# Sixteen multiplications of a cleared tile ahead of the first projection of a four-layer cross-attention kernel

## The chip, the cores and the metric

The kernel runs on one core of a Trainium2 chip. The core has a matrix engine (TensorE, PE in the profile), a vector engine (DVE), a scalar engine (ACT), GpSimd (POOL) and a sync engine (SP), which issues most of the DMAs. The metric is the device time of one execution in microseconds (us); lower is better.

## The reference

The input `x` is 128 sequences of 64 tokens of width 128, the context is 128 sequences of 64 tokens of width 256. Four cross-attention layers follow on one another, all over the same context. The first has 16 heads of width 64, a bias on four columns of the logits and an output bias; the other three have a norm ahead, 16 query heads of width 8 and 4 key and value heads. In short:

```python
# layer 0
q = x @ Wq; k = ctx @ Wk; v = ctx @ Wv                 # 128->1024, 256->1024, 256->1024
logits = einsum('bhqd,bhkd->bhqk', q, k) * 64 ** -0.5 + col_bias
x = softmax(logits) @ v  ->  reshape @ Wo + bo + x
# layers 1, 2, 3
xn = x * rsqrt(mean(x * x) + 1e-5) * norm_w
q = xn @ wq; k = ctx @ wk; v = ctx @ wv                # 128->128, 256->32, 256->32
x = x + softmax(q k^T / sqrt(8)) @ v @ wo
```

Everything is float32, in the reference and in the kernel.

## The kernel before, in words

The 128 sequences are cut into 32 groups of 4 (256 tokens each; `g` from 0 to 31). One group goes through all four layers in SBUF: `cT` holds its context transposed, `xT` its running output, `KT`, `V`, `K3`, `KB` and `VB` its keys and values, `QT` its queries, and four tiles `E[s][u]` of 128x512 its scores. Three groups are under way at a time (`s = g % 3`).

The work is cut into steps named `(kind, g, l, u)`: `k`, `v`, `k3`, `q0` are projections from the loaded inputs, `s` the scores, `t` the transposes of the softmax, `pv0` and `pv` the product with the values, `wo0` and `wo` the output projection, `x2` and `q` the norm and the query of a later layer. The order of these steps on each engine is written out by tables of numbers (`PE_TIME`, `ACT_TIME` and so on, sorted into `PE_ORDER`, `ACT_ORDER`, `DVE_ORDER`, `POOL_ORDER`, `SP_ORDER`). The engines meet at semaphores: an event such as `p_ev` counts the finished steps of a kind, and `w.wait_ge` waits for one. The change touches none of the tables.

At the start, SP issues the loads in this order: `cT` of group 0, three quarters of `wk0` (the key weights), `xq` of group 0, `wq0`, `wv` in parts, and then the rest. ACT issues the fourth quarter of `wk0` (quarter 1, the one that TensorE uses first) at L1054, then the token indices, `iota`, the masks `mk` and the identity. GpSimd clears `KB` and `VB`. The vector engine waits for the small loads of ACT's queue (`l_b`) and then computes the column bias (`vector_setup`, L1161 to L1174). TensorE starts with the four `k` steps of group 0 (L928), each 4 matmuls with a moving operand of 256 columns; the first of them waits for `cT` and for quarter 1 of `wk0`. Then come the `q0` steps (L955), two `v` steps (L940) and the scores (L966), on whose end the vector engine's first `add` (L1198) waits.

The program's matmul on float32 operands stands in the trace as two weight loads and two matmuls: the 16 of the `k` steps of group 0 are 32 rows there.

Of the kernel before, what the change touches and what calls it, by code (L numbers as in the profile page):

```python
# [671 lines left out]
def xattn_kernel(nc, t):  # L672
    with ExitStack() as ctx:
        def sb(name, shape, dt=F32):
            return ctx.enter_context(nc.sbuf_tensor(name, shape, dt))

        def of(order, *kinds):
            return [st for st in order if st[0] in kinds]

        def signal(name, events, inc=1):  # L680
            return Signal(ctx, nc, name, events, inc)

        psum = ctx.enter_context(nc.psum_tensor("psum", [128, 8, 512], F32))
# [25 lines left out]
        E = [[sb(f"E{s}_{u}", [128, 512]) for u in range(4)] for s in range(NS)]  # L709
# [36 lines left out]
        for st in of(PE_ORDER, *ON_ACT, *ON_DVE, "s", "t"):  # L746
            _, g, l, u = st
# [37 lines left out]
        d_setup = signal("d_setup", range(40))  # L785
        d_w = signal("d_w", range(3))
        g_one = signal("g_one", range(3))
        d_lr = signal("d_lr", of(DVE_ORDER, "lr"))
        p_ev = signal("p_ev", of(PE_ORDER, *ON_ACT, *ON_DVE))
        p_s = signal("p_s", of(PE_ORDER, "s"))  # L790
# [119 lines left out]

        def tensor_program(e):
            w = Engine(e)

            for st in PE_ORDER:
                kind, g, l, u = st
                s, at = g % NS, bank_of[st]
# [5 lines left out]
                if kind == "k":  # L922
                    w.wait_ge(l_c[g % NC], g)
                    w.wait_ge(l_wk[u], u)
                    for jj in range(2):
                        j = 2 * u + jj
                        for k in range(2):
                            m = e.matmul(bank[:, T * jj:T * jj + T], wk0[:, k, 128 * j:128 * j + 128], cTg[:, k, :],  # L928
                                         start=(k == 0), stop=(k == 1))
                    m.then_inc(p_ev.sem, 1)  # L930
                elif kind == "v":
# [7 lines left out]
                    for k in range(2):  # L939
                        m = e.matmul(bank[:, 0:hi - lo], cTg[:, k, 128 * p:128 * p + 128], wv[:, k, lo:hi],  # L940
                                     start=(k == 0), stop=(k == 1))
                    m.then_inc(p_ev.sem, 1)
                elif kind == "k3":
                    w.wait_ge(l_c[g % NC], g)
                    w.wait_ge(l_sm, 13)
                    for k in range(2):
                        m = e.matmul(bank[0:96, 0:T], wks[:, k, :, :].rearrange("p l n -> p (l n)"), cTg[:, k, :],  # L947
                                     start=(k == 0), stop=(k == 1))
                    m.then_inc(p_ev.sem, 1)
                elif kind == "q0":  # L950
                    w.wait_ge(l_xq[g % NX], g)
                    w.wait_ge(l_wq, "l_wq")
                    for jj in range(2):
                        j = 2 * u + jj
                        m = e.matmul(bank[:, T * jj:T * jj + T], wq0[:, 128 * j:128 * j + 128], xq[g % NX][:, :],  # L955
                                     start=True, stop=True)
                    m.then_inc(p_ev.sem, 1)
                elif kind == "s" and l == 0:
                    w.wait_ge(a_ev, *[("q0", g, 0, i) for i in range(4)])
                    w.wait_ge(a_ev, *[("k", g, 0, i) for i in range(4)])  # L960
                    for jj in range(4):
                        for b2 in range(2):
                            for par in range(2):
                                for h2 in range(2):
# [3 lines left out]
                                                 start=True, stop=True)  # L968
                    m.then_inc(p_s.sem, 1)
                elif kind == "s":  # L970
                    w.wait_ge(a_ev, ("q", g, l, u))
                    w.wait_ge(l_kb[l - 1][g % 2], (g, 15))
                    for p in halves(g, u):
                        for b2 in range(2):
                            for r in range(4):
# [5 lines left out]
                                             start=True, stop=True)  # L981
# [169 lines left out]
        def vector_setup(e, w):  # L1151

            n = [0]

            def then(m):
                m.then_inc(d_setup.sem, 1)
                e.wait_ge(d_setup.sem, n[0] + 1)
                n[0] += 1

            w.wait_ge(l_b, 6)  # L1160
            then(e.tensor_copy(idf[:, 0, :], idx[:, :]))  # L1161
            then(e.tensor_scalar(idf[:, 1, :], idf[:, 0, :], 0.0, 64.0, ALU.is_lt, ALU.mult))
            then(e.tensor_tensor(idf[:, 0, :], idf[:, 0, :], idf[:, 1, :], ALU.add))
            for i in range(4):
                then(e.tensor_scalar(eq[:, i, :], iota[:, :], idf[:, 0, i:i + 1], None, ALU.is_equal))
            then(e.tensor_tensor(eq[:, 0, :], eq[:, 0, :], eq[:, 1, :], ALU.max))
            then(e.tensor_tensor(eq[:, 2, :], eq[:, 2, :], eq[:, 3, :], ALU.max))
            then(e.tensor_tensor(eq[:, 1, :], eq[:, 0, :], eq[:, 2, :], ALU.mult))
            then(e.tensor_tensor(eq[:, 0, :], eq[:, 0, :], eq[:, 1, :], ALU.subtract))
            then(e.tensor_scalar(mk[:, :], mk[:, :], -1.0, 1.0, ALU.mult, ALU.add))  # L1170
            then(e.tensor_scalar(mk[:, :], mk[:, :], -20.0, None, ALU.mult))
            then(e.tensor_scalar(bias[:, :], eq[:, 0, :], mk[:, 0:1], None, ALU.mult))
            then(e.tensor_scalar(eq[:, 2, :], eq[:, 2, :], mk[:, 1:2], None, ALU.mult))
            then(e.tensor_tensor(bias[:, :], bias[:, :], eq[:, 2, :], ALU.add))  # L1174
            return n[0]
# [2 lines left out]

        def vector_program(e):
            w = Engine(e)  # L1180
            assert vector_setup(e, w) == setup_steps
            scaled = False
            for st in DVE_ORDER:
# [75 lines left out]
        @block.tensor  # L1259
        def _(e):  # L1260
            tensor_program(e)
# [5 lines left out]
        @block.vector  # L1267
        def _(e):
            vector_program(e)
# [38 lines left out]
```

## Time and profile before

| | |
|---|---|
| median of 3 runs | 1388.01 us (1386.95 to 1388.95) |
| the profiled execution's own time | 1385.33 us |
| its span, first to last instruction | 1383.5 us |
| TensorE busy | 1360.6 us (98%) |
| first matmul starts at | 4.52 us |

The page gives busy time by engine, the chain of work that ended last, and the costliest groups of instructions. In the trace, times count from the span's start. A matmul's duration runs from its start until its result is out, so the durations of matmuls that follow on one another overlap: 32 matmuls of 379 ns each do not take 32 times 379 ns. The pace is read from the starts, or from the chain, which gives the time without the overlap. The column PEclk is the granted clock of TensorE as a share of 2.4 GHz: 1.00 is 2.4 GHz, 0.50 is 1.2 GHz.

### The profile page before, as it was taken

What the parts mean: (1) busy time and instruction counts of PE and PEld (TensorE: products, weight loads), DVE (VectorE), ACT (ScalarE), POOL (GpSimd) and SP (SyncE); (2) the same over time, 40 slices, a digit from 0 to 9 for tenths busy, and PEclk for the clock granted to TensorE, in tenths of its full rate; (3) what the DMA queues carried; (4) which work ended last, traced back from release to release, by engine and by line L of the source; (5) the groups of instructions that cost most, each with busy time, mean ns of one, the idle gap of its engine ahead of it and who ended that gap; (6) DMA issues with size and microseconds to landing.
All of it is one profiled execution on the core that took longest, in us unless ns stands there. A gap on an engine that the chain in (4) does not pass through costs nothing.

```text
span 1383.5 us, 58994 instructions
## 1 busy us (share of the span) xinstructions
PE 1360.6 (98%) x25464; PEld 1053.6 (76%) x25464; DVE 1064.0 (77%) x2257; ACT 1003.3 (73%) x2207; POOL 735.7 (53%) x852
## 2 busy tenths in 40 slices
PE   8999999999999999999999999999999999999996
PEld 6777777778777777777777777777777777777775
DVE  3488777977778877778877779777788777787876
ACT  3677777767777677777677777677776776767785
POOL 5355446555456545466554465455565544655643
PEclk9999999999999999999999999999999999999998
DMA  5010000110000010100101101100011011010000
GB/s 149 18 30 18 19 25 23 27 27 24 26 21 24 27 27 23 28 18 26 27 24 26 29 17 27 27 23 27 18 27 27 23 27 31 12 39 19 7 22 13
DMA packets 46003, 37.02 MB, mean 27 GB/s; under 512 B 17072, under 2 KB 41520, under 8 KB 45744
## 3 DMA queue, kind: packets, MB, share of 16 engines
q1 hardware_dynamic: 44576, 32.89, 8.9%
q8 instruction: 201, 3.29, 1.0%
q14 instruction: 58, 0.48, 0.1%
q10 hardware_dynamic: 1168, 0.36, 0.1%
HBM read 16.42 MB, written 4.19 MB: 15 GB/s over the span
## 4 chain that ended last, share of the span: by engine, by line
PE 94%; DVE 3%; ACT 2%; issue 1%; POOL 0%; DMA 0%; DVEq 0%; POOLq 0%
PE psum L940 18%; PE psum L928 16%; PE psum L995 10%; PE psum L1013 8%; PE psum L955 8%; PE psum L977 7%; PE psum L1041 7%; PE psum L1005 5%; PE psum L966 5%; PE psum L1049 4%; PE psum L1018 3%; PE psum L947 2%; PE psum L1024 2%; ACT E L1127 1%; DVE st L1211 1%
## 5 line engine op out<-in xcount | busy, mean ns | idle before, releaser
L887 POOL TENSOR_TENSOR E<-E,st 128x512 f32<-128x512 f32 x488 | 497.1, 1043 | 169.8 <-DVE st L1223 161.8
L1122 ACT ACTIVATE E<-E,inv 128x512 f32<-128x512 f32 x384 | 273.4, 722 | 136.7 <-DVE E L1215 135.3
L1211 DVE TENSOR_REDUCE st<-psum 128x8 f32<-128x512 f32 x372 | 240.2, 672 | 147.9 <-PE psum L977 147.7
L1220 DVE TENSOR_REDUCE st<-E 128x8 f32<-128x512 f32 x488 | 320.9, 664 | 34.1 <-ACT E L1115 27.1
L1127 ACT COPY E<-psum 128x512 f32<-128x512 f32 x512 | 275.1, 609 | 36.5 <-PE psum L995 36.3
L940 PE MATMUL psum<-wv,cT 128*128 128x374 f32 (+1 forms) x768 | 273.3, 486 | 0.0
L1215 DVE TENSOR_TENSOR E<-psum,st 128x512 f32<-128x512 f32 x372 | 248.1, 676 | 0.3
L928 PE MATMUL psum<-cT,wk 128*128 128x256 f32 x1024 | 241.9, 384 | 5.4 <-DMA wk<-in_L_xattn_Wk 4.5
L899 POOL TENSOR_TENSOR nt<-nt,powers 128x2 f32<-128x2 f32 (+1 forms) x102 | 19.9, 195 | 422.2 <-DVE nt L1250 401.4
L928 PEld LDWEIGHTS psum<-cT,wk 128*128 128x128 f32 x1024 | 192.7, 191 | 39.9 <-DMA cT<-in_ctx_t 4.5
L940 PEld LDWEIGHTS psum<-wv,cT 128*128 128x128 f32 x768 | 138.1, 189 | 73.2 <-ACT V L1083 8.5
L995 PE MATMUL psum<-ident,E 64*128 64x64 f32 x4096 | 157.4, 226 | 7.8 <-ACT E L1122 4.0
L883 POOL TENSOR_TENSOR E<-E,st 128x512 f32<-128x512 f32 x140 | 142.6, 1043 | 36.5 <-DVE st L1205 24.6
L995 PEld LDWEIGHTS psum<-ident,E 64*128 64x128 f32 x4096 | 138.8, 139 | 24.4 <-issue 12.6
L955 PE MATMUL psum<-xq,wq 128*128 128x256 f32 x512 | 129.0, 385 | 0.0
L1041 PEld LDWEIGHTS psum<-E,VB 128*32 128x32 f32 x6144 | 92.1, 110 | 37.4 <-issue 14.8
L1013 PE MATMUL psum<-QT,wo 128*128 128x256 f32 (+1 forms) x544 | 119.1, 372 | 0.0
L1083 ACT COPY V<-psum 128x374 f32<-128x374 f32 (+1 forms) x192 | 87.3, 457 | 42.7 <-PE psum L940 41.9
L1107 ACT ACTIVATE QT<-psum 128x512 f32<-128x512 f32 x128 | 75.9, 599 | 56.0 <-PE psum L955 47.7
L955 PEld LDWEIGHTS psum<-xq,wq 128*128 128x128 f32 x512 | 94.8, 190 | 23.1 <-issue 10.8
L977 PE MATMUL psum<-KB,QT 32*64 32x256 f32 x3072 | 109.7, 388 | 2.1 <-ACT QT L1146 1.0
L1041 PE MATMUL psum<-E,VB 128*32 128x64 f32 x6144 | 108.2, 221 | 0.4 <-ACT E L1127 0.2
(63 smaller groups left out, 1612.3 us busy)
## 6 DMA issues: line engine op xcount, KB each, us to landing
KB<-K SPq DMA_DIRECT2D x1536, 8.0 KB
cT<-in_ctx_t SPq DMA_DIRECT2D x32, 256.0 KB, 2.8
xq<-in_x_t SPq DMA_DIRECT2D x32, 128.0 KB, 2.1
out<-xT SPq DMA_DIRECT2D x30, 128.0 KB, 1.8
wk<-in_L_xattn_Wk SPq DMA_DIRECT2D x3, 256.0 KB, 5.6
wv<-in_L_xattn_Wv SPq DMA_DIRECT2D x2, 374.0 KB, 8.6
wq<-in_L_xattn_Wq SPq DMA_DIRECT2D x1, 512.0 KB, 7.6
wo<-in_L_xattn_Wo SPq DMA_DIRECT2D x1, 512.0 KB, 4.3
```

What stands on the lines that cost most here:

```text
L887: e.tensor_tensor(E3, E3, wide(stat[s][u][:, 16:24]), ALU.mult).then_inc(g_nrm.sem, 1)
L928: m = e.matmul(bank[:, T * jj:T * jj + T], wk0[:, k, 128 * j:128 * j + 128], cTg[:, k, :], start=(k == 0), stop=(k == 1))
L940: m = e.matmul(bank[:, 0:hi - lo], cTg[:, k, 128 * p:128 * p + 128], wv[:, k, lo:hi], start=(k == 0), stop=(k == 1))
L955: m = e.matmul(bank[:, T * jj:T * jj + T], wq0[:, 128 * j:128 * j + 128], xq[g % NX][:, :], start=True, stop=True)
L995: m = e.transpose(psum[:, at[2 * n + i], c:c + 64], E[s][2 * p + r][rows, 128 * k:128 * k + 128], ident[rows, rows])
L1013: m = e.matmul(bank[:, tokens], wo0[:, j, :], QT[s][:, j, tokens], start=(j == 0), stop=(j == 7))
L1041: m = e.matmul(bank[32 * r:32 * r + 32, 64 * b:64 * b + 64], VBg[:, b, c:c + 32], E[s][b][:, n:n + 64], start=(gp == 0), stop=(gp == 1))
L1122: e.activation(E[s][u][:, :], E[s][u][:, :], ACT.Exp, scale=inv[s][:, u // 2:u // 2 + 1]).then_inc(a_exp.sem, 1)
L1127: e.copy(E[s][u][:, :], psum[:, i, :]).then_inc(a_et.sem, 1)
L1211: e.tensor_reduce(stat[s][u][:, 0:8].rearrange("p (r h) -> p r h", r=2), scores_of[g, l, u], AX, ALU.max).then_inc(d_max.sem, 1)
L1215: e.tensor_tensor(pairs(E[s][u][:, :]), scores_of[g, l, u], stat[s][u][:, 0:8].rearrange("p (r h a) -> p r h a", r=2, a=1).to_broadcast([1 ...
L1220: e.tensor_reduce(stat[s][u][:, 8:16], heads(E[s][u][:, :]), AX, ALU.add).then_inc(d_sum.sem, 1)
```

## The change

The vector engine clears the first 128 columns of tile `E[0][0]` as its first instruction, and says so by a new semaphore `d_blank`. TensorE waits for it and then multiplies this 128x128 float32 piece by itself sixteen times, into the first 128 columns of PSUM bank 7. Nobody reads that result; the next matmul that is put into this bank starts afresh, and the first step that writes `E[0][0]` (the `add` of group 0) comes after TensorE's scores of group 0. Everything else stays.

```diff
@@ -785,6 +785,7 @@
         d_w = signal("d_w", range(3))
         g_one = signal("g_one", range(3))
+        d_blank = signal("d_blank", ["blank"])
@@ -910,7 +911,10 @@
         def tensor_program(e):
             w = Engine(e)
-
+            blank = E[0][0][:, 0:128]
+            w.wait_ge(d_blank, "blank")
+            for _ in range(16):
+                e.matmul(psum[:, 7, 0:128], blank, blank, start=True, stop=True)
             for st in PE_ORDER:
@@ -1178,6 +1182,7 @@
         def vector_program(e):
             w = Engine(e)
+            e.memset(E[0][0][:, 0:128], 0.0).then_inc(d_blank.sem, 1)
             assert vector_setup(e, w) == setup_steps
```

On TensorE, at the program's start, this stands before (`cT` is the context, `wk` the key weights; `l_wk1`, `l_wk2`, `l_wk0` are the landings of quarters of `wk`, `l_c0` that of `cT`):

```order
L1259 UNCONDITIONAL_BRANCH [waits barrier_Pool_Activation_PE_DVE_SP_release]
L928 MATMUL psum<-cT,wk 128x256 [waits l_wk1,l_c0]
L928 MATMUL psum<-cT,wk 128x256 x3
L928 MATMUL psum<-cT,wk 128x256 [waits l_wk2]
L928 MATMUL psum<-cT,wk 128x256 x3
```

And on TensorE at the same place with the change (`E_0` is the cleared tile; lines are 4 further down, and L932 is L928 of before):

```order
L1264 UNCONDITIONAL_BRANCH [waits barrier_Pool_Activation_PE_DVE_SP_release]
L917 MATMUL psum<-E_0 128x128 [waits d_blank]
L917 MATMUL psum<-E_0 128x128 x15
L932 MATMUL psum<-cT,wk 128x256 [waits l_wk1,l_c0]
L932 MATMUL psum<-cT,wk 128x256 x3
L932 MATMUL psum<-cT,wk 128x256 [waits l_wk2]
```

Sixteen matmuls now stand ahead of the wait for the loads; the order behind them is the same.

On the vector engine, at the program's start, before (`l_b` is the landing of the small loads; `idf` holds the token indices as floats):

```order
L1267 UNCONDITIONAL_BRANCH [waits barrier_Pool_Activation_PE_DVE_SP_release]
L1161 CAST idf<-idx 128x4 [waits l_b]
L1162 TENSOR_SCALAR idf<-idf 128x4 [waits d_setup]
```

And there with the change:

```order
L1272 UNCONDITIONAL_BRANCH [waits barrier_Pool_Activation_PE_DVE_SP_release]
L1185 MEMSET E_0 128x128
L1165 CAST idf<-idx 128x4 [waits l_b]
L1166 TENSOR_SCALAR idf<-idf 128x4 [waits d_setup]
```

The clearing stands ahead of the engine's wait for the loads and waits for nothing itself.

## Rows read from the trace of the kernel before

**Rows 1.** The page: busy time, share of the span, instructions; then the chain by engine.

```profile
PE 1360.6 (98%) x25464; PEld 1053.6 (76%) x25464; DVE 1064.0 (77%) x2257; ACT 1003.3 (73%) x2207; POOL 735.7 (53%) x852
...
PE 94%; DVE 3%; ACT 2%; issue 1%; POOL 0%; DMA 0%; DVEq 0%; POOLq 0%
```

**Rows 2.** The chain of waits, 0 to 40 us: start us, us, what.

```profile
0.74 3.64 DMA wk<-in_L_xattn_Wk
4.38 0.14 issue
4.52 8.63 PE psum L928 x32
13.15 3.45 PE psum L955 x16
16.60 2.51 PE psum L940 x8
19.11 1.14 PE psum L966 x64
...
20.35 1.29 DVE E L1198 x2
```

**Rows 3.** Timeline of TensorE, 0 to 22 us: start us, us, group [idle before].

```profile
4.52 8.63 PE L928 MATMUL psum<-cT,wk 128*128 128x256 f32 x32 [4.52 <-DMA wk<-in_L_xattn_Wk]
12.99 3.62 PE L955 MATMUL psum<-xq,wq 128*128 128x256 f32 x16
16.44 2.68 PE L940 MATMUL psum<-wv,cT 128*128 128x374 f32 x8
19.05 2.10 PE L966 MATMUL psum<-KT,QT 64*64 64x64 f32 x128
```

**Rows 4.** Line L928, 4 to 6 us: duration ns min/median/max, first and last start.

```profile
L928 PE MATMUL psum<-cT,wk x4: 634/634/764, 4.5 to 5.9; 128*128 128x256 f32 x4
```

**Rows 5.** Line L928, 7.4 to 7.8 us.

```profile
L928 PE MATMUL psum<-cT,wk x3: 380/544/634, 6.8 to 7.6; 128*128 128x256 f32 x3
```

**Rows 6.** Line L928, 8.2 to 8.6 us.

```profile
L928 PE MATMUL psum<-cT,wk x3: 379/379/379, 8.0 to 8.5; 128*128 128x256 f32 x3
```

**Rows 7.** Stretches: length, PE busy (instructions), PEclk, DMA share, GB/s.

```profile
0.00:4.52 4.52, 0.00 (x1) 1.00 0.59 167
4.52:5.52 1.00, 1.00 (x3) 1.00 0.28 72
```

**Rows 8.** The chain, 1290 to 1297 and 1330 to 1337 us, 128x128 moving operands.

```profile
1292.88 3.77 PE psum L1013 x32
```

**Rows 9.** Stretches at the end, columns as in rows 7.

```profile
1363.00:1370.00 7.00, 5.82 (x174) 1.00 0.07 21
1370.00:1372.30 2.30, 0.25 (x13) 1.00 0.00 0
1372.30:1373.86 1.56, 0.73 (x17) 0.68 0.00 0
1373.86:1378.77 4.91, 4.91 (x144) 0.50 0.03 7
1378.77:1380.25 1.48, 0.00 (x1) 0.69 0.00 0
...
1379.60:1379.70 0.10, 0.00 (x0) 0.55 0.00 0
```

**Rows 10.** Waits, 0 to 25 us: who waited for whom, us, times, longest.

```profile
DVE idf L1161 <- DMA mk<-in_mask_S_fk: 12.3, 1, 12.3
ACT KT L1075 <- PE psum L928: 4.2, 1, 4.2
DVE E L1198 <- PE psum L966: 4.0, 1, 4.0
```

**Rows 11.** Timeline of all engines, 0 to 22 us, as rows 3.

```profile
0.74 0.48 ACTq L1054 DMA_DIRECT2D wk<-in_L_xattn_Wk  x1
0.79 0.14 POOL L865 MEMSET ones<- 128x48 f32 x1
3.18 0.43 SPq L814 DMA_DIRECT2D wq<-in_L_xattn_Wq  x1
4.13 2.14 SPq L816 DMA_DIRECT2D wv<-in_L_xattn_Wv  x1
15.79 0.26 DVE L1173 TENSOR_SCALAR eq<-eq,mk 128x64 f32<-128x64 f32 x1
17.79 0.64 ACT L1075 COPY KT<-psum 128x512 f32<-128x512 f32 x1
```

**Rows 12.** DMA issues: KB each, median us from issue to landing.

```profile
wv<-in_L_xattn_Wv SPq DMA_DIRECT2D x2, 374.0 KB, 8.6
wq<-in_L_xattn_Wq SPq DMA_DIRECT2D x1, 512.0 KB, 7.6
```

**Rows 13.** The page's groups: out<-in xcount | busy, mean ns of one.

```profile
L872 POOL MEMSET KB<- 128x1024 f32 x6 | 5.4, 961 | 0.1
```

## The prediction

> **What bounds the kernel now.** I read four views, from the whole to the start. First the page: TensorE is busy for 98% of the span and 94% of the chain that ended last lies on it, while no other engine is over 77% [rows 1]. Whatever the change does must be done to TensorE's time. The change adds to the first microseconds and touches no table of the order, so the second view is the chain of waits of the first 40 us [rows 2]. The chain begins with a DMA, quarter 1 of wk, from 0.74 to 4.38 us. Then TensorE carries it without a break: the 32 matmuls of the key projection to 13.15, the query projection to 16.60, the values to 19.11, and half of the scores, whose end lets the vector engine start at 20.35. The wait list says the same from the other side: the vector engine had stood idle for 4.0 us when the scores came, and ACT for 4.2 us when the first keys came [rows 10]. So in this stretch a microsecond on TensorE is a microsecond of the kernel, both ways, and from 0.74 to 4.38 TensorE has nothing to do.
>
> The third view is the durations within the key projection. Its first matmuls take 634 to 764 ns each [rows 4], those after 8 us take 379 ns [rows 6], and the change from one to the other falls between the last long one, started at 6.8, and the first short one, started at 7.6 [rows 5]. The work is the same shape throughout. The pace shows what this is worth. The 16 matmuls of the query projection, same shape, take 3.45 us in the chain [rows 2], 0.216 us each. At that pace 32 of them would take 6.90 us. They took from 4.52 to 12.99, the start of the next group [rows 3], 8.47 us. The first ones therefore cost 8.47 - 6.90 = **1.57 us too much**. If a slow one takes twice the time (0.431 us), 1.57 / 0.216 = 7.3 of them were slow, which fills 7.3 x 0.431 = 3.1 us and ends at 7.6, where rows 5 has the change. So TensorE ran at 1.2 GHz for about 3.1 us from its first matmul and at 2.4 GHz from then on. A trap for the reader: the granted clock is printed as 1.00 in these very stretches [rows 7]; here the durations have to be believed. Where the clock column does move is the fourth view, the end of the kernel: after a stretch in which TensorE was at work for only 0.25 of 2.30 us, the clock fell to 0.50 and stayed there while TensorE was busy without a gap from 1373.86 to 1378.77; it came back at 1379.65 or so, 5.8 us after that work began [rows 9]. The two places give the two ends for how long work goes on at half clock: 3.1 and 5.8 us.
>
> **The change, part by part.**
>
> *The clearing on the vector engine.* One memset of 128x128. Nothing of this shape runs there before. From below, GpSimd's memset of 128x48 takes 0.14 us; the nearest on the vector engine is 0.26 us for 128x64 [rows 11]; from above, GpSimd's memset of eight times the width takes 0.96 us [rows 13]. I take 0.2 us, between the two nearest. The engine's next instruction waits until 12.3 us anyway [rows 10], so on that engine it costs nothing. The queues start at 0.74 [rows 11]; with 0.2 for the clearing and the 0.14 us that passed between the landing of wk and the first matmul [rows 2], the first added matmul starts at about 1.1 us (1.0 to 1.9 by the ends).
>
> *The sixteen matmuls.* They become 32 rows of weights 128x128 and 128 moving columns. This shape does stand in the trace: in the last groups' output projection, 32 such matmuls take 3.77 us at full clock [rows 8], 0.118 us each. That is more than half of 0.216: with so few columns the pace is not that of the columns alone, so I use this row and not half of the wider one. At half clock I take twice that, 0.236 us (if only the columns count it is 0.216). All at full clock they would take 3.8 us and end at 4.9; all at half clock 7.5 us and end at 8.7. The wait that they fill ends at 4.52. So they do not fit into the wait in either case; this is the central point of the sum.
>
> *The clock.* I take the same 3.1 us of work at half clock as before. It fits 3.1 / 0.236 = 13.1 of the 32; the clock is up at 1.1 + 3.1 = 4.2 us. The other 18.9 take 18.9 x 0.118 = 2.2 us. The added block ends at 1.1 + 3.1 + 2.2 = **6.4 us**.
>
> *The key projection.* It starts at 6.4 in place of 4.52, 1.9 us later, and runs at full clock: 6.90 us in place of 8.47, 1.57 us less. It ends at 13.3 in place of 12.99. **Sum: +1.9 - 1.57 = +0.3 us.**
>
> The Trainium skill, in "TensorE: Matmul & The Clock Gate", section "Part 1: The HAM clock gate", says that the array starts at half rate and that activity releases it, and that the warm-up is a budget of time, not of a number of matmuls. The trace agrees as far as it goes (3.1 us slow in rows 4 to 6). By this rule the change does not save the slow time but only spends it on work that nobody needs, and what is gained is only as much of it as lies in the wait; by a reading in which a number of matmuls (7 of them) releases the clock, it would be up at 1.1 + 7.3 x 0.236 = 2.8 us, the block would end at 2.8 + 24.7 x 0.118 = 5.7 us, and the sum would be -0.4 us.
>
> *What is late next.* A start 0.3 us later is carried on: the chain from L928 to the vector engine's add has no gap [rows 2]. If the projection ended earlier instead, two things could hold it: wq lands at 3.18 + 7.6 = 10.8 us and the second part of wv at 4.13 + 8.6 = 12.7 [rows 11, 12], needed at 12.99 and 16.44 [rows 3], so 1.6 us earlier would still do; and ACT's last copy of keys ends at 18.43 [rows 11], 0.6 us ahead of the scores, and moves with TensorE. So gain or loss reaches the scores whole. From there the same order runs with the same durations, and I give the remaining 1360 us no change.
>
> Against the profiled execution's own 1385.33 us (span 1383.5 and 1.8 around it) this makes 1385.6. The median of the runs shown is 2.7 us above the profiled execution, so the forecast on that scale is 1388.01 + 0.3 = **1388.3 us**. A measurement of this kernel can tell about 0.2%, 2.8 us, from no change; the forecast is a tenth of that.
>
> **The rivals.**
>
> *B, the clock comes late.* The end of the kernel shows 5.8 us of work at half clock before it rose [rows 9], and the rise may also be bound to the moment of 7.6 us and not to the work. With 5.8 us, 24.6 of the added matmuls are slow and 7.4 take 0.9 us: the block ends at 7.8, the projection at 14.7, +1.7 us. With a rise at 7.6, 27.5 slow and 4.5 fast: it ends at 8.1, +2.0 us. Against it: nothing says that the start is like the end. Time 1389.7 to 1390.0.
>
> *C, the other side: zeros do not raise the clock.* The change would then not do what it says. All 32 are slow, the block ends at 1.1 + 7.5 = 8.6 us, the key projection starts 4.1 us late and is as slow at first as before: **+4.1 us**, 1392.1, slower by 0.30%. It decides as soon as the block is slow to its end and the first real matmuls still take over 600 ns. For it: no row shows what zeros do. Against it: the durations of this trace change after a time of work on a fixed shape, and I know of no row in which the data mattered. The same page of the Trainium skill says in that section that all-zero operands do not trip another limiter, one for peak current with three or more busy cores; by it zeros change nothing on one core, and no run here shows that limiter.
>
> *D, the block fits.* If the added matmuls were done by 4.5 us with the clock up, the whole 1.57 us would be gained: 1386.4. It needs 32 matmuls in 3.4 us, 0.106 each from the first on, below the 0.118 of full clock [rows 8]. A part of it remains possible (a shape whose weights do not change may go faster than in rows 8; the clock may rise earlier): -0.4 to -1.6 us.
>
> *E, something further down the line.* 64 more instructions lie ahead on TensorE and 1% of the chain is issue [rows 1], so that small gaps elsewhere may fall differently, by up to some 3 us either way.
>
> **How the numbers follow.** Forecast (-0.4 to +1.0 us) 0.60; B 0.17; C 0.08; D 0.09; E 0.06. Faster by over 0.2% needs 2.8 us, more than all the slow time at the start holds; only E can give it: 0.04 with what I may have missed. Slower by over 0.2%: C nearly whole, and a share of E: 0.09. Within 0.2%: 0.87. The range takes in D whole and B whole and leaves out C; with the spread of the runs (about 1 us each way) that is 1385.8 to 1391.2.
>
> **What the changed profile would show.** A group of 32 matmuls at L917 from about 1.1 us; its durations long at first and short from about 4.2 us; the key projection (L932 there) starts at about 6.4 us with a median and maximum near 379 ns, and takes some 7.1 us in place of 8.63; the query projection starts at 13.3; the vector engine's first add at about 20.7 in place of 20.35. B shows a start of the key projection near 8 us; C shows it at 8.6 with durations of 634 ns; D shows it at 4.5. The forecast is wrong if the add's start moves by over 1 us, or if it does not move and the total does.

## The result, and the profile after

The changed kernel takes 1390.3 us in the median of 17 runs (1387.83 to 1392.93); the kernel before took 1387.55 in 17 runs beside it (1383.38 to 1388.95). The ratio is **1.0023, with a 95% interval from 1.0017 to 1.0030**: slower by 3.2 us (the two medians are 2.75 us apart). The forecast was 1388.3 with a range from 1385.8 to 1391.2. The time lies in the range, but the step up is ten times the +0.3 us of the sum. It stands just above the 0.2% from which the prediction called a time slower, the class that had been given 0.09; the interval reaches below that line.

The profiled execution of the changed kernel took 1392.03 us, its span is 1390.2, 6.7 us over that of before. Both profiled executions are unlike their medians, in opposite directions (1385.33 against 1387.55, 1392.03 against 1390.3), so that their difference overstates the change.

The start of the chain of waits of the changed kernel (start us, us, what); it answers to [rows 2]:

```profile
0.83 0.18 DVE E L1185
1.01 0.04 issue
1.05 6.72 PE psum L917 x32
7.77 6.91 PE psum L932 x32
14.68 3.45 PE psum L959 x16
18.13 2.51 PE psum L944 x8
20.64 1.14 PE psum L970 x64
...
21.88 1.29 DVE E L1203 x2
```

The clearing takes 0.18 us and the first added matmul starts at 1.05. The block takes 6.72 us and not 5.3. The key projection behind it takes 6.91 us, all at full clock, in place of 8.63. The first add starts at 21.88 in place of 20.35, 1.53 us later.

The durations in the block tell when the clock rose. Line L917 of the changed kernel, first from 6.4 to 7 us and then from 7.15 to 7.5 (duration in ns min/median/max, first and last start):

```profile
L917 PE MATMUL psum<-E x5: 348/421/421, 6.1 to 7.0; 128*128 128x128 f32 x5
```

```profile
L917 PE MATMUL psum<-E x6: 274/275/421, 6.8 to 7.5; 128*128 128x128 f32 x6
```

Until about 7.1 us each added matmul takes 421 ns, from then on 275. The engine had worked at 1.2 GHz for 6.1 us, in place of the 3.1 us of the profile before. It had seen nothing but zeros until then, so zeros do raise the clock.

That is 1.5 of 6.7 us. The rest is further down the line. The time that TensorE stood idle with nothing to release it (engine, line, "issue": us in total, times, longest) in the profile before, and then in the changed one:

```profile
PE psum L995 <- issue: 2.0, 4, 0.7
PE psum L1005 <- issue: 1.3, 3, 0.8
PE psum L977 <- issue: 0.6, 2, 0.5
```

```profile
PE psum L1045 <- issue: 2.5, 2, 1.5
PE psum L1009 <- issue: 2.4, 6, 0.7
PE psum L999 <- issue: 1.4, 3, 0.7
PE psum L981 <- issue: 0.6, 1, 0.6
PE psum L944 <- issue: 0.5, 1, 0.5
```

Together 3.9 us before and 7.4 after, and at other places. One such place lies inside a row of 32 equal matmuls. First the timeline of before, where the 32 follow on one another, then the same step of the changed kernel, which stops after 27:

```profile
73.95 1.12 PE L977 MATMUL psum<-KB,QT 32*64 32x256 f32 x32
```

```profile
75.48 1.10 PE L981 MATMUL psum<-KB,QT 32*64 32x256 f32 x27
77.19 0.65 PE L981 MATMUL psum<-KB,QT 32*64 32x256 f32 x5 [0.61 <-issue]
```

The kernel before has such places too. At this one the changed kernel has none. Timeline of before:

```profile
152.84 0.73 PE L1005 MATMUL psum<-E,V 64*64 64x64 f32 x33
154.38 0.69 PE L1005 MATMUL psum<-E,V 64*64 64x64 f32 x31 [0.81 <-issue]
```

and the same step of the changed kernel:

```profile
156.11 1.16 PE L1009 MATMUL psum<-E,V 64*64 64x64 f32 x64
```

A semaphore cannot be the cause in the midst of one step, since only its first matmul waits. What the places have in common shows when TensorE's rows (weight loads, matmuls and its own semaphore rows) are counted from the start of the trace, the first as 0. The matmul behind a gap of this kind of over 0.25 us is row 4801, 15042, 20674, 32450, 38082, 43714, 47554 or 50370 before, and row 1986, 4033, 9665, 20674, 21442, 27074, 38082, 38850, 46017, 46273 or 51138 after. Two of them stand in both lists (20674 with 0.25 and 0.62 us, 38082 with 0.26 in both). Divided by 256, each leaves 193 or 194, and so do all 116 gaps of this kind in the 14 profiles of this document. And the program's code is itself loaded by DMA, in 201 pieces. The page of the changed kernel, DMA queues (packets, MB, share of 16 engines):

```profile
q8 instruction: 201, 3.29, 1.0%
```

3.29 MB in 201 packets is 16 KB each; TensorE has about 51,500 rows, which is 201 times 256. At the gap before 77.19 us a piece of code came in between 74.42 and 75.81, and TensorE went on 1.4 us after that; at the one before 154.38 of the old profile, between 151.70 and 153.01, again 1.4 us ahead. In all 116 gaps it is 1.0 to 1.6 us. So I read the gaps like this: where a boundary between two pieces falls behind many short instructions, TensorE arrives at it before its code does. The change puts 64 rows ahead of everything (16 matmuls, each two weight loads and two matmuls), so that every later boundary falls 64 rows earlier in the program. That became theory 2, against theory 1, that only the start counts.

### The profile page after: what moved, and what is told of

The parts are those of the page before. It is cut to its first block, busy times and chain, and to the rows that moved or that the text cites. A ratio compares the mean times of both kernels' runs of the same rounds, so it can differ in the third digit from the quotient of the medians.

```text
span 1390.2 us, 59059 instructions
## 1 busy us (share of the span) xinstructions
PE 1366.8 (98%) x25496; PEld 1059.7 (76%) x25496; DVE 1065.2 (77%) x2258; ACT 1003.2 (72%) x2207; POOL 736.4 (53%) x852
## 3 DMA queue, kind: packets, MB, share of 16 engines
q8 instruction: 201, 3.29, 1.0%
## 4 chain that ended last, share of the span: by engine, by line
PE 94%; DVE 2%; ACT 2%; issue 1%; DMA 1%; POOL 0%; DVEq 0%; POOLq 0%
PE psum L944 17%; PE psum L932 16%; PE psum L999 10%; PE psum L1017 8%; PE psum L959 8%; PE psum L981 7%; PE psum L1045 7%; PE psum L1009 5%; PE psum L970 4%; PE psum L1053 4%; PE psum L1022 3%; PE psum L951 2%; PE psum L1028 1%; ACT E L1131 1%; ACT E L1126 1%
## 5 line engine op out<-in xcount | busy, mean ns | idle before, releaser
L932 PE MATMUL psum<-cT,wk 128*128 128x256 f32 x1024 | 240.2, 382 | 1.5 <-DMA cT<-in_ctx_t 1.5
L932 PEld LDWEIGHTS psum<-cT,wk 128*128 128x128 f32 x1024 | 191.6, 190 | 35.7 <-ACT K L1105 1.4
```

## Experiments

Each ratio is to the kernel before, timed beside it on the same chip: experiments 1 to 4 on one chip, 5 to 8 on a second, 9 to 12 on a third. Ratios of different chips meet only through the kernel before. "Tiny" stands for a matmul with 32x32 weights and 1 moving column: it puts the same four rows into the stream and takes little time (32 rows in 1.86 us, in experiment 2).

**1. The clearing and the wait alone.** Against the changed kernel:

```diff
-            for _ in range(16):
-                e.matmul(psum[:, 7, 0:128], blank, blank, start=True, stop=True)
```

> The clearing and TensorE's wait for it stay, the sixteen matmuls are gone. Theory 1 (only the start counts: the added block ends late and pushes the key projection back): no block, ratio to before 1.000, key projection starts at 4.5 us. Theory 2 (the 64 added rows in TensorE's stream shift all later code against the places, every 256 rows, at which code loading stalls it): no rows added, ratio 1.000 as well, idle time put down to issue 3.9 us as before. If it is slower by over 0.1%, the clearing or the wait costs and both are short of something.

Measured: ratio 1.0002 (0.9993 to 1.0011). The clearing and the wait cost nothing that the runs can tell. The profile taught something else, though. Its chain:

```profile
4.47 9.73 PE psum L930 x32
```

The key projection took 9.73 us here, 8.63 before, with nothing ahead of it in either. So the time at half clock is not the same in each execution; twice the excess over full clock, (9.73 - 6.91) x 2, is 5.6 us here, and (8.63 - 6.91) x 2 = 3.4 us before. And the issue idle time was 5.6 us, not 3.9, so one profile does not fix it to better than 2 us.

**2. Sixteen tiny ones.**

```diff
-                e.matmul(psum[:, 7, 0:128], blank, blank, start=True, stop=True)
+                e.matmul(psum[0:32, 7, 0:1], blank[0:32, 0:32], blank[0:32, 0:1], start=True, stop=True)
```

> The same 64 rows in TensorE's stream, but each matmul only 32x32 weights and 1 moving column, so that the block is over long before the loads land at 4.4 us. Theory 1: ratio 1.000, first add of the vector engine at 20.4 us. Theory 2: first add at 20.4 us too, but the stalls fall as in the changed kernel: TensorE's idle time put down to issue near 7 us in place of 3.9, ratio 1.001 to 1.002.

Measured: ratio **1.0022** (1.0013 to 1.0030), as much as the whole change. In its timeline the block is over at 2.9 us and the key projection starts on time:

```profile
1.05 1.86 PE L917 MATMUL psum<-E 32*32 32x1 f32 x32 [1.05 <-DVE E L1185]
4.45 2.04 PE L932 MATMUL psum<-cT,wk 128*128 128x256 f32 x4 [1.53 <-DMA wk<-in_L_xattn_Wk]
```

The issue idle time is 7.1 us, near the 7.4 of the changed kernel. Theory 1 is out: the key projection is not pushed back and the 3 us are there.

**3. Eight of the sixteen.** `range(16)` becomes `range(8)`.

> Eight of the sixteen matmuls: 16 rows at 0.21 us end at 4.5 us, just as the loads land; 32 rows are added to the stream. If the clock rises by work done (3.1 us of it), the key projection runs at full clock at once and the first add comes 1.5 us earlier than before (18.9 us). If it rises at a moment near 7.1 to 7.5 us whatever was done, the first add stays at 20.4. Theory 1: the ratio follows the add alone, 0.999 or 1.000. Theory 2: plus a change of the stalls for a shift of 32 rows, of either sign up to 2 us.

Measured: ratio 0.9990 (0.9981 to 1.0000). The first add starts at 19.37 us, the earliest of all, though not as early as the 18.9 expected for a clock that rises after 3.1 us of work. A load that the prediction did not name now holds TensorE for a moment, that of the output bias `bo`; the profiles of experiments 7 and 12 show it too, at 0.2 us:

```profile
21.81 1.10 PE L951 MATMUL psum<-cT,wks 128*96 128x256 f32 x4 [0.20 <-DMA bo<-in_L_xattn_bo]
```

**4. Ones in place of zeros.**

```diff
-            e.memset(E[0][0][:, 0:128], 0.0).then_inc(d_blank.sem, 1)
+            e.memset(E[0][0][:, 0:128], 1.0).then_inc(d_blank.sem, 1)
```

> The changed kernel with the tile set to 1.0 in place of 0.0. If zeros count as little work for the clock, the clock rises earlier than at 7.1 us, the block takes under 6.7 us and the kernel gains up to 1.5 us on the changed one. If the values do not matter, the block takes 6.7 us again and the ratio is that of the change, 1.002.

Measured: ratio 1.0021 (1.0012 to 1.0031), as with zeros. In the profiled execution the clock did rise earlier, at 4.2 us, and the block took 5.33 us, but experiment 1 has shown that this moment differs from execution to execution; the runs show no gain. The profile is worth its line, because it is the case that the prediction had worked out (block over at 6.4):

```profile
1.05 5.33 PE psum L917 x32
6.38 6.91 PE psum L932 x32
13.29 3.45 PE psum L959 x16
```

**5. Eight tiny ones.** As 2, with `range(8)`.

> Eight tiny matmuls (32x32 weights, 1 moving column) at the start: the 32 added rows of the eight-matmul kernel without its work. If that kernel's ratio of 0.999 came from the clock, this one stands at 1.000 or above; if it came from where the code boundaries fall with a shift of 32 rows, this one shows 0.999 too.

Measured: ratio 0.9991 (0.9982 to 1.0000). A shift of 32 rows seems to be a small gain by itself (the interval just reaches 1; experiment 11 gives 0.9992), so experiment 3 had not shown that the clock was its cause.

**6. Sixteen tiny ones at the end.** No block at the start; behind TensorE's last step:

```diff
+            w.wait_ge(d_ev, PE_ORDER[-1])
+            for _ in range(16):
+                e.matmul(psum[0:32, 7, 0:1], blank[0:32, 0:32], blank[0:32, 0:1], start=True, stop=True)
```

> The 64 rows of the sixteen tiny matmuls stand behind TensorE's last step in place of ahead of its first, after the vector engine's last result. Theory 2 (code position) says that no earlier instruction changes its place: ratio 1.000, stalls at the same rows as before. If the ratio is 1.002 again, it is the longer program as such, or its additional fetches, and not the position.

Measured: ratio 1.0003 (0.9993 to 1.0013). The same 64 rows cost nothing that the runs can tell where nothing stands behind them. It is what the rows stand ahead of, and not the length of the program.

**7. Two wide ones.**

```diff
-            for _ in range(16):
-                e.matmul(psum[:, 7, 0:128], blank, blank, start=True, stop=True)
+            wide_blank = blank.rearrange("p (a n) -> p a n", a=1).to_broadcast([128, 4, 128])
+            for _ in range(2):
+                e.matmul(psum[:, 7, :].rearrange("p (a n) -> p a n", a=4), blank, wide_blank, start=True, stop=True)
```

> Two matmuls with 512 moving columns (the cleared 128 repeated four times): 4 matmul rows at 0.85 us each at half clock, done at about 4.5 us as in the eight-matmul kernel, but only 8 rows are added to the stream. Theory 1 and 2 together: the clock part of the gain is there (first add on average 1.5 us earlier), and the shift is small; ratio 0.999, at best 0.998.

Measured: ratio 1.0005 (0.9993 to 1.0017). A miss. The start is as expected (block over at 4.7, first add at 19.56), but the gain is not in the total. Either a shift of 8 rows costs something, or the gain at the start was lost on the way; a shift of 8 rows without work was not run.

**8. Thirty-two tiny ones.** `range(32)`.

> Thirty-two tiny matmuls at the start, 128 rows added, done at about 4.6 us. Theory 2: stalls at other matmuls again; the sum of them differs from both before and the shift of 64. From the spacing of the instructions before I expect a shift of 128 to be as bad as that of 64 or worse: 1.002 to 1.003. Theory 1 (start only): 1.000.

Measured: ratio 1.0021 (1.0012 to 1.0031), as expected.

**9. Forty tiny ones.** `range(40)`. The shift was chosen from the spacing of TensorE's rows in the profiles, as the worst.

> Forty tiny matmuls, 160 rows added, done at about 5.3 us, 0.8 us after the loads. From the spacing of TensorE's rows in the profiles so far (256 rows to a piece of code, a stall where the 150 to 160 rows ahead of a boundary run in under 2.4 us) a shift of 160 rows is the worst of all: 4 to 6 us of stalls more than with no shift. Theory 2: ratio 1.003 to 1.005. Theory 1, the start only: 0.8 us, 1.0006.

Measured: ratio **1.0034** (1.0022 to 1.0046, from 6 runs where the others have 11 or 12), the highest of all, though the interval overlaps those of experiments 2 and 8. The 4 to 6 us of added gaps are not in its profile: the issue idle time is 6.8 us there, against 3.9 to 6.2 with no shift. The first add in its profile is at 21.25 us, within what kernels without a block show (below). The block ends at 5.4, some 0.9 us after the loads have landed, and more than that the start cannot explain.

**10 and 11. Eight real and eight tiny ones, beside each other.**

> The eight-matmul kernel once more, now beside its twin with eight tiny matmuls on the same chip. The profiles so far give the first add at 19.4 to 19.6 us where work fills the wait and at 20.4 to 22.2 where it does not, 1.7 us apart in the mean. If that is carried to the end, this kernel is 0.0012 below its twin; if it is lost on the way, they are equal.

> The twin: the same 32 rows without work. Theory 2: 0.999 again, from the place of the code alone, and 0.0012 above the kernel with eight real matmuls if the clock part is carried to the end.

Measured: **0.9978** (0.9970 to 0.9987) with the real ones, 0.9992 (0.9983 to 1.0002) with the tiny ones, 0.0014 or 1.9 us apart (the medians are 1382.62 and 1384.86 us). Their first adds (vector engine's timeline; the eight real ones first, then the tiny ones):

```profile
20.23 1.29 DVE L1203 TENSOR_TENSOR E<-psum,bias 128x512 f32<-128x512 f32 x2 [3.83 <-PE psum L970]
```

```profile
21.48 0.69 DVE L1203 TENSOR_TENSOR E<-psum,bias 128x512 f32<-128x512 f32 x1 [5.17 <-PE psum L970]
```

The two adds are 1.25 us apart, and the two spans, 1381.1 and 1382.4 us, still 1.3, with issue idle times of 3.5 and 3.3 us: in this pair of profiles the gain at the start is carried to the end. Eight real ones beat the kernel before here. The same pair in experiments 3 and 5 stood at 0.9990 and 0.9991, but on two chips. Taken together the real ones are ahead by 0.0008, about as much as the uncertainty of such a difference; that the clock part reaches the end is likely and not settled.

**12. Six of the sixteen.** `range(6)`.

> Six real matmuls, 24 rows added, done at 3.6 us, so that 0.9 us of the wait stays idle. By the spacing of the rows a shift of 24 is about as good as none (-0.5 us); the clock part is somewhat under that of eight, since the clock comes after work begun at 1.05 us and may count the idle stretch: -1.2 us. Ratio 0.999 (0.998 to 1.000).

Measured: ratio 1.0006 (0.9996 to 1.0016). A miss like experiment 7: the start has its gain (first add at 19.47), the total has not. My reading of the rows had the highest ratio at the shift of 160, as it came out, within the noise said above; it does not predict the small shifts.

The two parts, side by side. Position, from the kernels whose added rows do no work (experiments 1, 6; 5, 11; 2; 8; 9):

| rows ahead of the first step | 0 | 32 | 64 | 128 | 160 |
|---|---|---|---|---|---|
| ratio | 1.0002, 1.0003 | 0.9991, 0.9992 | 1.0022 | 1.0021 | 1.0034 |
| issue idle in the profiles, us | 5.6, 6.2 (before: 3.9) | 6.1, 3.3 | 7.1 | 7.1 | 6.8 |

Start, from the moment of the first add in each profile:

| what fills the wait | first add, us | mean |
|---|---|---|
| nothing, or tiny ones over by 2.9 (before, 1, 2, 5, 6, 11) | 20.35, 21.40, 21.11, 20.51, 22.23, 21.48 | 21.2 |
| six or eight real ones, or two wide ones (3, 7, 10, 12) | 19.37, 19.56, 20.23, 19.47 | 19.7 |
| sixteen real ones (the change, 4) | 21.88, 20.49 | 21.2 |

Experiments 8 and 9 stand in no row: their key projections start late, at 5.08 and 5.40 us (in 8 behind a load, in 9 behind the block), with the first add at 21.83 and 21.25. Within a row the adds lie up to 1.9 us apart, so the mean of two says little.

## Why the prediction was right or wrong

**The number.** That the time lies in the range is luck. The range reached that high because it took in rival B, a late clock, and the spread of the runs; what filled it was another mechanism. (Its ends are also not quite those of the sum: 1386.4 - 1 and 1390.0 + 1 are 1385.4 and 1391.0.) By the sign that the prediction gave for itself, an add that moves by over 1 us, the forecast was wrong in the first profile already, with 1.53 us.

**The place.** Right that TensorE bounds the start without a gap, that the clearing is free (0.2 us taken, 0.18 measured; experiment 1), that the first added matmul starts at about 1.1 us (1.05), and that the block does not fit into the wait while half of it would.

**The pace of the shape.** Close, by errors that cancel. In experiment 4, with the clock rising at 4.2 us, the block ended at 6.38 and the key projection at 13.29, and the sum had 6.4 and 13.3. But the starts in that block lie 0.213 us apart at half clock, not the doubled 0.236 that I took, and 0.111 to 0.112 at full clock, not 0.118. Two single steps are longer and make up for it: 0.38 us from the first start to the second, and 0.22 from the last to the key projection. So 3.77 / 32 of rows 8 is not the pace either: such a stretch holds the time to the last result too.

**The clock.** The step "I take the same 3.1 us of work at half clock as before" was wrong for the changed kernel's profile, where it was 6.1 us, and that is rival B's +1.7 us (1.53 measured). But rival B is no property of the change. The kernels that have no work ahead show key projections of 8.63, 9.73 and more; the profile before was the best case that I have of them, and I took one execution's value for a constant. In the table the sixteen matmuls change the mean of the first add by nothing (21.2 and 21.2), near the +0.3 that the sum had for equal clocks; with two executions that scatter by 1.4 us this is not shown. That a longer time at half clock costs the real matmuls as much as the added ones is argued. A rise after a fixed number of matmuls, which the prediction priced at -0.4 us, is out: some 7 were slow before, 14 in experiment 4 and 27 in the change.

**Zeros.** Rival C is refuted by the block of the change, whose durations fall from 421 to 275 ns while only zeros had been multiplied; experiment 4, with ones, has the same ratio.

**The failed step** is "From there the same order runs with the same durations, and I give the remaining 1360 us no change". The runs put +0.0022, 3 us, in its place: experiment 2 has it without pushing the key projection back, experiment 6 loses it when the rows stand at the end. It is the mechanism that rival E hinted at (64 more instructions ahead, up to 3 us either way) with a chance of 0.06. I had no row for it, because I had not asked where the 3.9 us of issue idle time lay; the gaps in the midst of a step would have shown it.

**What stays open.** The gaps at the boundaries account for part of the 3 us only: the issue idle times of the three profiles with 64 rows (7.4, 7.1, 5.2) are 1.3 us above those of the three with none (3.9, 5.6, 6.2) in the mean. The spans of the same six profiles are only 2.0 us apart in the mean (1390.2, 1388.5, 1385.1 against 1383.5, 1386.2, 1388.0). Each profile is one execution and they scatter by 2 us and more, so the rest may be small delays that this sum does not hold, or scatter. That the rows ahead cost 3 us is shown; that they do it through the places at which code is loaded fits every gap, and how much of the 3 us this makes is open. A version whose 64 rows leave the boundaries where they were, 256 rows added ahead, was not tried: that many rows do not fit into the wait. And the ratio for shifts of 8 and 24 rows without work is not known.

## What to carry to other kernels

When TensorE is the bound and its code is long, adding instructions ahead of the main part moves all of the code against the boundaries at which it is loaded; here such additions without work changed the time by -0.09 to +0.34%, and what the added work itself did was 0.14% at most. Test such an edit against a twin with the same number of instructions and no work, and look for idle time without a releaser in the midst of a step. Work that is to raise the clock has something to gain only as far as it fits into the wait: six or eight matmuls, or two wide ones, ended by then and had their first add 1.5 us earlier in the mean, sixteen did not fit and show no gain.

## What the runs showed of the hardware

TensorE was held up at rows that leave 193 or 194 on division by 256, for up to 1.46 us, and went on 1.0 to 1.6 us after a 16 KB piece of its code had come in (all 116 gaps of over 0.25 us in 14 profiles). From the start of the first matmul with 128x128 weights the clock stayed at 1.2 GHz for 3.0 to 6.2 us, differently in executions of like kernels (3.0 before, 6.1 in the change, 3.15 in experiment 4; 6.2 in experiment 6, whose key projection took 10.02 us from its start to that of the next group in place of 6.90; twice the excess is the time at half clock), while the granted clock was printed as 1.00 throughout; only the durations and the starts show it.
